# A state-space scan with attention and experts on one core: the chunk's head reordered, row scales stored once and loaded, the weights loaded in three groups

## What is computed

```python
xn = layernorm(x)                                   # mean and variance of each row
out = x + ssm(xn) + ffn(xn)                         # ffn: latent attention, then 7 experts, top 2

def ssm(x):                                         # D_MODEL 256, D_INNER 512, D_STATE 16
    x_in, z = split(x @ W_in)
    x_in = silu(causal_conv4(x_in, W_conv) + b_conv)
    dbc = x_in @ W_xproj                            # 64 columns for dt, 16 for B, 16 for C
    dt = softplus(dbc[:64] @ W_dt + b_dt)
    A = -exp(A_log)
    for t in range(512):
        state = clip(state * exp(clip(dt_t * A)) + x_t * dt_t * B_t, -10, 10)
        y_t = sum_n(state * C_t) + D * x_t
    return (y * silu(z)) @ W_out
```

## Time and profile before

| | us |
|---|---|
| median of three runs (4593.74 to 4607.09) | 4605.54 |
| profiled execution | 4602.04 |
| its span, first to last instruction | 4600.0 |
| span before the state-space part (first row load of it at 2195.09) | 2195 |
| first scan step | 2262.1 |
| end of the scan of chunk 30, start of that of chunk 31 | 4513.7 |

### The profile page before, as it was taken

The page is one execution under the profiler, slowest core; times in us unless marked ns, Lnnn a source line. Parts: engine busy times, 40 slices in busy tenths (PEclk is TensorE's granted clock), DMA queues, the critical chain, the costliest instruction groups (busy, mean ns, idle before and its releaser), DMA issues.

```text
span 4600.0 us, 72135 instructions
## 1 busy us (share of the span) xinstructions
PE 3800.7 (83%) x22840; PEld 2863.4 (62%) x22840; DVE 3006.1 (65%) x5613; ACT 2500.9 (54%) x6473; POOL 2243.8 (49%) x1251
## 2 busy tenths in 40 slices
PE   5888888888888857999588888888888888888886
PEld 2444444444444436777477777777777777777776
DVE  4445554454545322222399998888998989888887
ACT  1434444443434422333477776767767677776774
POOL 2233233333323220000376776777777777776774
PEclk8889999999989878999799999999999999999998
DMA  3222223322322216666222221222222222221221
GB/s 94 88 75 86 91 76 95 95 85 76 100 76 76 74 44 204 209 204 210 80 72 84 75 81 71 81 75 84 72 75 86 75 76 80 75 85 68 81 80 36
DMA packets 268587, 419.76 MB, mean 91 GB/s; under 512 B 60245, under 2 KB 232662, under 8 KB 245656
## 3 DMA queue, kind: packets, MB, share of 16 engines
q1 hardware_dynamic: 255896, 380.98, 25.7%
q0 software_dynamic: 12288, 33.57, 2.1%
HBM read 330.56 MB, written 83.10 MB: 90 GB/s over the span
## 4 chain that ended last, share of the span: by engine, by line
PE 16%; POOL 13%; ACT 9%; DVE 7%; issue 6%; DMA 1%; DVEq 0%; SPq 0%; POOLq 0%; ACTq 0%
POOL m_ub L1534 10%; PE m_Y L1902 7%; ACT m_dA L1652 6%; PE m_Y L1912 2%; PE m_F L1867 2%; PE m_F L1856 2%; DVE m_PR L1756 2%; POOL m_yg L1544 1%; DVE m_PR L1764 1%; DVE m_S L1756 1%; DVE m_S L1764 1%; PE m_Y L1915 1%; POOL m_dtx L1513 1%; PE m_F L1875 1%; DVE m_ub L1741 1%
## 5 line engine op out<-in xcount | busy, mean ns | idle before, releaser
L1534 POOL TENSOR_TENSOR m_ub<-m_Bb,m_dtx 128x2048 f32<-128x2048 f32 x256 | 1156.7, 4542 | 482.8 <-PE m_Y L1902 476.2
L1652 ACT ACTIVATE m_dA<-m_dt,m_a_neg 128x128 f32<-128x128 f32 x4096 | 1210.0, 389 | 27.3 <-DVE m_S L1764 23.4
L1902 PE MATMUL m_Y<-m_ub,m_ident 128*128 128x128 f32 x8192 | 1026.8, 290 | 222.1 <-DVE m_ub L1741 205.3
L1902 PEld LDWEIGHTS m_Y<-m_ub,m_ident 128*128 128x128 f32 x8192 | 1007.2, 206 | 232.0 <-DVE m_ub L1741 213.6
L531 ACT ACTIVATE f_pt<-f_X 128x512 f32<-128x512 f32 (+1 forms) x704 | 371.5, 554 | 723.4 <-PE f_X L822 692.0
L607 DVE TENSOR_REDUCE f_nm<-f_Y 128x1 f32<-128x512 f32 (+3 forms) x896 | 433.5, 530 | 364.5 <-PE f_Y L816 361.3
L1756 DVE SCALAR_TENSOR_TENSOR m_PR<-m_dA,m_S 128x512 f32<-128x512 f32 x512 | 355.8, 695 | 207.6 <-ACT m_dA L1652 84.0
L815 PE MATMUL f_Y<-f_kst,f_qst 96*128 96x512 bf16 (+3 forms) x1024 | 286.4, 335 | 104.9 <-DVE f_nm L607 87.8
L1756 DVE SCALAR_TENSOR_TENSOR m_S<-m_dA,m_PR 128x512 f32<-128x512 f32 x512 | 354.8, 693 | 12.0
L1764 DVE CUSTOM_DVE_ANT_1 m_S<-m_S,m_ub 128x512 f32<-128x512 f32 x512 | 353.3, 690 | 0.0
L1764 DVE CUSTOM_DVE_ANT_1 m_PR<-m_PR,m_ub 128x512 f32<-128x512 f32 x512 | 353.1, 690 | 0.2 <-DVE m_PR L1756 0.2
(11 more groups left out here) (238 smaller groups left out, 6622.9 us busy)
## 6 DMA issues: line engine op xcount, KB each, us to landing
m_Bb<-m_bc_dram SPq DMA_DIRECT2D x64, 1024.0 KB, 4.7
m_Cb<-m_bc_dram SPq DMA_DIRECT2D x64, 1024.0 KB, 4.7
f_parts_dram<-f_parts SPq DMA_DIRECT2D x32, 768.0 KB, 4.1
f_kst<-f_parts_dram SPq DMA_DIRECT2D x192, 128.0 KB, 2.6
f_qst<-f_parts_dram SPq DMA_DIRECT2D x192, 128.0 KB, 2.6
e_rows<-sorted_rows SPq DMA_DIRECT2D x70, 256.0 KB, 2.8
e_wg<-Wg SPq DMA_DIRECT2D x70, 256.0 KB, 2.9
e_wu<-Wu SPq DMA_DIRECT2D x70, 256.0 KB, 4.0
```

What stands on the lines that cost most here:

```text
L1534: pool.tensor_tensor(ub[:, h, i, :, :], Bb[:, s, :, :], dtx[:, par, m, None, s * SN:(s + 1) * SN].to_broadcast([P, NST, SN]), ALU.mult).th ...
L1652: last = act.activation(dA[:, h, i, n, :], dtt[:, par, m, s * SN:(s + 1) * SN], ACT.Exp, scale=a_neg[:, m, n:n + 1])
L1902: last = pe.matmul(Y[:, i * SN:(i + 1) * SN], ident[:, :], ub[:, h, i, n, :], start=False, stop=(n == NST - 1), skip_group_check=True)
```

## The change

The row scales (1 over the deviation, and minus the mean times that) are no longer worked out in the state-space part. `build_attn` has them already in `mvx`; SP stores them for every sequence (item `mvs`), and `load_x` loads them with the rows, two numbers a row. `stats` and `rstd_of` go. `load_x` is moved from the head of SP's chunk into `spread_bc`, three chunks ahead.

`project` is cut in two, `project_a` (the second half of x and the first of z, into F[2] and F[3]) and `project_b` (into F[1] and F[0]); `conv` is done in halves, the second half first. TensorE's list is now: sum of the last unit, `dbc`, `transposes`, output product, `dt_proj`, sum of unit 0, `project_a`, sum of unit 1, `project_b`, first half of `conv`, sum of unit 2, second half of `conv`. `transposes` write to F[0], and the output product goes to F[2] in place of Y. On ScalarE `normalise` stands first, and `evac_T` and the decays of unit 2 stand ahead of softplus. On VectorE silu comes at steps 3 and 4, the residual add at step 1 of unit 1, and `log_rest` at step 0 of unit 2. A new semaphore `d_done` tells `silu_x` that the skip term has read x2.

In the setup the loads have three semaphores: w_in, the columns for conv and skip, and the six others.

```diff
+            if kind == "mvs":
+                dst = at(rows_stat, b)
+                held(xn_done, 2 * b + 1)
+                with nc.allow_non_contiguous_dma(reason="two numbers of a row"):
+                    sp.dma_start(dst, mvx[:, :, :]).then_inc(mv_stored, 16)
...
-                dve.tensor_copy(mvx[:, 0, :], sc1[:, 1, :])
-                dve.tensor_copy(mvx[:, 1, :], sc1[:, 9, :]).then_inc(xn_done, 1)
+                dve.wait_ge(mv_stored, 16 * b)
+                dve.tensor_copy(mvx[:, :, 0], sc1[:, 1, :])
+                dve.tensor_copy(mvx[:, :, 1], sc1[:, 9, :]).then_inc(xn_done, 1)
...
+            with nc.allow_non_contiguous_dma(reason="two numbers of a row"):
+                sp.dma_start(rowsc[:, :, :], stat_tm[bass.ds(rows, CN), :].rearrange("(j p) d -> p j d", p=P)).then_inc(x_loaded, 16)
+
+        def spread_bc(c, ahead):
             for s in range(NSUB):
...
             for s in range(NSUB):
+                if s == NSUB - 1 and ahead is not None:
+                    load_x(ahead)
                 held(u_ready[2 * s + 1], 2 * c)
                 sp.dma_start(Bb[:, s, :, :], bc_dram[s:s + 1, 0, :, :].to_broadcast([P, NST, SN])).then_inc(b_loaded[s], 16)
...
         def chunk(c, par, rows_ahead=True):
-            if rows_ahead:
-                load_x(c + 2)
             store(c - 1)
             load_res(c)
             load_info(c + 1, 1 - par)
-            spread_bc(c + 1)
+            spread_bc(c + 1, c + 3 if rows_ahead else None)
 
         load_x(0)
-        load_info(0, 0)
+        sp.dma_start(w_in[:, :, :], W_in.rearrange("(k p) n -> p k n", p=P)).then_inc(w_in_loaded, 16)
+        with nc.allow_non_contiguous_dma(reason="per-channel columns, once"):
+            for k in range(TAPS):
+                sp.dma_start(w_cv[:, k, :], W_conv[k, :].rearrange("(m p) -> p m", p=P)).then_inc(cols_loaded, 16)
+            sp.dma_start(d_col[:, :], D.rearrange("(m p) -> p m", p=P)).then_inc(cols_loaded, 16)
         for dst, src in loads:
             sp.dma_start(dst, src).then_inc(w_loaded, 16)
-        with nc.allow_non_contiguous_dma(reason="per-channel columns, once"):
-            for k in range(TAPS):
-                sp.dma_start(w_cv[:, k, :], W_conv[k, :].rearrange("(m p) -> p m", p=P)).then_inc(w_loaded, 16)
-            sp.dma_start(d_col[:, :], D.rearrange("(m p) -> p m", p=P)).then_inc(w_loaded, 16)
+        load_info(0, 0)
         load_x(1)
-        spread_bc(0)
-        load_x(2)
+        spread_bc(0, 2)
...
-        def rstd_of(c):
-            pool.wait_ge(stats_done, TT * (c + 1))
-            pool.tensor_tensor(veps[:, :], mv[:, :, 1], eps[:, :], ALU.add).then_inc(veps_done, 1)
-            pool.wait_ge(veps_done, c + 1)
...
         def normalise(c):
-            act.wait_ge(shift_done, c + 1)
             act.wait_ge(xT_done, c)
-            act.wait_ge(x_loaded, 16 * (c + 1))
+            act.wait_ge(x_loaded, 32 * (c + 1))
             for j in range(TT):
-                act.activation(xn[:, j, :], xm[:, j, :], ACT.Identity, scale=rstd[:, j:j + 1],
-                               bias=shift[:, j:j + 1]).then_inc(xn_done, 1)
+                act.activation(xn[:, j, :], xm[:, j, :], ACT.Identity, scale=rowsc[:, j, 0:1],
+                               bias=rowsc[:, j, 1:2]).then_inc(xn_done, 1)
 
         def evac_T(c):
             act.wait_ge(xT_done, c + 1)
             act.wait_ge(xz_done, 4 * c)
-            act.activation(xnT[:, :, :], F[2][:, :, :], ACT.Copy).then_inc(xnT_ready, 1)
-
-        def evac_x(c):
+            act.activation(xnT[:, :, :], F[0][:, :, :], ACT.Copy).then_inc(xnT_ready, 1)
+
+        def evac_xz(c):
             act.wait_ge(conv_done, 2 * c)
             act.wait_ge(xpad_ready, 2 * c)
-            act.wait_ge(ident_ready, 5)
+            act.wait_ge(ident_ready, 4)
             if not isinstance(c, int) or c > 0:
 
                 act.activation(xpad[:, :, 0:HALO], xpad[:, :, CN:CN + HALO], ACT.Copy).then_inc(halo_done, 1)
                 act.wait_ge(halo_done, c)
             for i in range(2):
-                act.wait_ge(xz_done, 4 * c + i + 1)
-                act.activation(xpad[:, 2 * i:2 * i + 2, HALO:HALO + CN], F[1 + i][:, :, :], ACT.Copy).then_inc(xpad_ready, 1)
-
-        def tanh_z(c):
-            for i in range(2):
-                act.wait_ge(xz_done, 4 * c + 3 + i)
+                hx = 1 - i
+                act.wait_ge(xz_done, 4 * c + 2 * i + 1)
+                act.activation(xpad[:, 2 * hx:2 * hx + 2, HALO:HALO + CN], F[1 + hx][:, :, :], ACT.Copy).then_inc(xpad_ready, 1)
+                act.wait_ge(xz_done, 4 * c + 2 * i + 2)
...
-        act.wait_ge(setup_neg, 2)
         normalise(0)
         evac_T(0)
-        evac_x(0)
-        tanh_z(0)
+        act.wait_ge(w_loaded, 16 * 6)
+        act.activation(a_neg[:, :, :], a_neg[:, :, :], ACT.Exp).then_inc(setup_neg, 1)
+        evac_xz(0)
         tanh_x(0)
+        normalise(1)
         evac_dbc(0)
+        evac_T(1)
         softplus(0)
         ln(0)
+        act.wait_ge(setup_neg, 2)
         decays(0, 0, 0)
-        normalise(1)
-        evac_T(1)
-        evac_x(1)
-        tanh_z(1)
+        decays(0, 0, 1)
+        evac_xz(1)
         tanh_x(1)
-        decays(0, 0, 1)
 
         def body(c, par, first, last):
+            if has(c + 2):
+                normalise(c + 2)
+            if first:
+                decays(c, par, 2)
             if not last:
                 evac_dbc(c + 1)
+            if has(c + 2):
+                evac_T(c + 2)
+            if not first:
+                decays(c, par, 2)
+            if not last:
                 softplus(c + 1)
-            if has(c + 2):
-                normalise(c + 2)
-            decays(c, par, 2)
-            if not last:
                 ln(c + 1)
-                if has(c + 2):
-                    evac_T(c + 2)
             weigh(c, par)
             decays(c, par, 3)
+            if has(c + 2):
+                evac_xz(c + 2)
             if not last:
-                if has(c + 2):
-                    evac_x(c + 2)
-                    tanh_z(c + 2)
                 decays(c + 1, 1 - par, 0)
                 if has(c + 2):
                     tanh_x(c + 2)
...
-        def stats(c):
-            dve.wait_ge(x_loaded, 16 * (c + 1))
-            for j in range(TT):
...
-        def silu_x(c, par, halves=(0, 1)):
+        def silu_x(c, par, halves=(1, 0)):
             if not isinstance(c, int) or c >= 2:
-                dve.wait_ge(nsum_done[NU - 1], 2 * (c - 1))
+                dve.wait_ge(d_done, c - 1)
             for i in halves:
-                dve.wait_ge(thx_ready, 2 * c + i + 1)
+                dve.wait_ge(thx_ready, 2 * c + (1 - i) + 1)
...
-            dve.tensor_tensor(ot[:, :, :], Y[:, :].rearrange("p (j d) -> p j d", j=TT), res[:, :, :], ALU.add).then_inc(ot_done, 1)
...
+            dve.tensor_tensor(ot[:, :, :], F[2][:, :, :], res[:, :, :], ALU.add).then_inc(ot_done, 1)
...
             slots = [dict() for _ in range(NU)]
             if not first:
                 slots[0][5] = lambda: gate_y(c - 1, 1 - par, NU - 1)
-                slots[1][0] = lambda: add_res(c - 1)
+                slots[1][1] = lambda: add_res(c - 1)
             for u in range(1, NU):
                 slots[u][6] = lambda u=u: gate_y(c, par, u - 1)
             if not last:
-                slots[0][6] = lambda: silu_x(c + 1, 1 - par, [0])
-                slots[0][7] = lambda: silu_x(c + 1, 1 - par, [1])
-                slots[1][7] = lambda: log_rest(c + 1)
-            if has(c + 2):
-                slots[0][3] = lambda: stats(c + 2)
+                slots[1 if first else 0][3] = lambda: silu_x(c + 1, 1 - par, [1])
+                slots[1 if first else 0][4] = lambda: silu_x(c + 1, 1 - par, [0])
+                slots[2][0] = lambda: log_rest(c + 1)
...
         def transposes(c):
             pe.wait_ge(xn_done, TT * (c + 1))
-            pe.wait_ge(x2_ready, 2 * c)
+            if not isinstance(c, int) or c > 0:
+                pe.wait_ge(z_copied, 2 * c)
             for k in range(KM):
                 for j in range(TT):
-                    last = pe.transpose(F[2][:, k, j * P:(j + 1) * P], xn[:, j, k * P:(k + 1) * P], ident[:, :])
+                    last = pe.transpose(F[0][:, k, j * P:(j + 1) * P], xn[:, j, k * P:(k + 1) * P], ident[:, :])
             last.then_inc(xT_done, 1)
 
-        def project(c):
+        def project(c, i):
+            for m in range(2):
+                blk = 2 * i + m
+                for k in range(KM):
+                    last = pe.matmul(F[(1 + i) % 4][:, m, :], w_in[:, k, blk * P:(blk + 1) * P], xnT[:, k, :],
+                                     start=(k == 0), stop=(k == KM - 1))
+            last.then_inc(xz_done, 1)
+
+        def project_a(c):
             pe.wait_ge(xnT_ready, c + 1)
-            for i in range(4):
-                if i == 0:
-                    pe.wait_ge(sp_low, c)
-                if i == 1:
```

(84 more changed lines are left out.)

122 lines of the change are left out of this document (47 added, 75 removed).

## The result

The changed kernel took **4430.4 us** (median of 4 runs, 4412.2 to 4434.9) against 4601.9 us (median of 4 runs of the kernel before beside it): the ratio is 0.9606, with a 95% interval from 0.9574 to 0.9637. The forecast was 4441 us. The profiled execution of after took 4428.2 us, with a span of 4426.1.

A forecast was written before the change was run, and what follows sets the result against it. VectorE's scan, its own instructions plus its waits, was taken to bound the loop. Loop −134, start −12, first chunk −11 and last chunks and end −8 made −165 from 4602, plus 3.5: 4441 us, range 4398 to 4530.

The forecast's parts named there:

- The loop, −134 forecast: 28 looped chunks: 65.3 work, 1.35 wait ahead of unit 2, 1.2 edge; 67.8 us each against 72.6.
- with nothing to spare: Chunk's end: GpSimd's inputs of the next unit 0 end at +65.9, VectorE wants them at +66.1; the 1.10 us wait goes.
- it takes 7.3 like the sum at 3019.29: Chunk head, TensorE: sum of unit 3 starts at +1.4, takes 7.3 us and ends at +8.8.
- 1.2 edge: Chunk boundary: the loop's jump back, about 2.4 us at every second boundary, stays; 1.2 us per chunk on average.
- Rival B: TensorE at half clock ahead of the output product, or edge delays: 1.5 to 1.6 us more per chunk, 4486 us; chance 0.2.
- The start, −12 forecast: Setup: with three load groups x rows come first and conv starts 13.4 us earlier, less 1.3; 12 us taken.
- They now run ahead while VectorE waits: First chunk: projection and conv of chunk 1 no longer stand between its units; 70 us instead of 81.4, −11.
- Chunk 29 on, −8 forecast: Last three chunks and the end: no projection there; the head of each saves 2 to 3 us, −8.
- Ahead of the state-space part, 0 forecast: Attention part: 16 stores of small row-scale rows cost 0, bounds 0 to +10 us; no gain possible.
- D: Slower: late transposes (+18, not +12) hold the output product and unit 2; 73.7 us a chunk, 4662 us at 8 us; chance 0.04.
- E: The wait ahead of unit 2 vanishes too, or the edge is partly hidden: 38 us less, 4403 us; chance 0.06.
- C: GpSimd becomes the bound, late at unit 2 and the next unit 0: 70.4 us a chunk, 4512 us; chance 0.1.

The follow-up runs named there:

- e3: Changed kernel with TensorE running the output product ahead of dbc and the transposes again, as before: 4552.8 us, ratio 0.991.
- e5: Changed kernel with ScalarE's softplus of the next chunk ahead of the decays of unit 2 again: 4468.9 us, ratio 0.9728.
- e8: Changed kernel with skip-term matmuls repeated (six more times in unit 1, four in unit 3) to keep TensorE busy: 4416.9 us, ratio 0.9597.
- e4: Changed kernel with the old setup: all engines wait for every load, TensorE for all diagonals: 4466.0 us, ratio 0.9706.
- e10: Changed kernel with ScalarE's projection copies for chunk 1 ahead of the first decays, tanh_x between them: 4432.8 us, ratio 0.9644.
- e2: Changed kernel without the stored row scales: statistics worked out in the state-space part again, attention part as before: 4458.7 us, ratio 0.9702.
- e12: e11 with log_rest moved back to step 7 of unit 1: 4361.5 us, ratio 0.9515.
- e7: Changed kernel with four chunks per hardware loop pass instead of two, 7 jumps back instead of 14: 4426.5 us, ratio 0.9636.
- e11: Changed kernel with the edits of e7, e8 and e10 together: 4385.2 us, ratio 0.9547.

## Why the prediction was right

**The loop, −134 forecast, −137.1 measured.** (Unrounded, 28 times 72.57 less 67.85 is 132.) By its terms, from the step times of chunks 2 to 27: the work of 65.3 came to 65.0. Unit 2 waits 0.76 us and not 1.35: the 0.7 us that I added in every second chunk for a late ScalarE and TensorE behind the jump didn't come. The decays end 7.5 us early in every chunk, and GpSimd's inputs at +33.3 in either kind. The end of a chunk costs 1.46 and not 1.2: 28 × 0.26 = 7 us for GpSimd, which I had at +65.9 against VectorE's +66.1 "with nothing to spare", and which is at +66.1 in fact. Two waits of 0.2, at the end of units 0 and 2, were not in the sum. The errors, −0.3 and −0.6 against +0.26 and +0.4, nearly cancel: 67.8 forecast, 67.67 measured.

**The chain.** dbc's end was forecast at +11.7 and is +12.1 in the median; the decays of unit 2 at +16.6 to +26 ran from +16.55 to +26.0; the inputs of unit 2 at +24.6 to +33.6 ran from +24.3 to +33.3; the sum of unit 2 starts at +52.7 for +53.0, and the inputs of the next unit 0 run from +57.1 to +66.1 for +56.9 to +65.9. The residual add waits no more. e3 shows that this chain is the cause. e5 shows that the new place of the decays adds 19.3 us; without it 117.8 of the 137.1 us are still there.

**A step that failed at a small price:** "it takes 7.3 like the sum at 3019.29", of the sum of unit 3. It takes 8.7 us on average (9.04 in chunk 10), because the clock is often low behind its gap at the boundary, which I hadn't priced. Behind a jump back the gap is 3.4 to 4.8 us, and all 13 of these sums are slow (8.8 to 10.3 us). Elsewhere it is 2.0 to 2.4 us, and 5 sums of 15 are slow; in chunk 2 the same gap as in chunk 10 was followed by a sum at full speed.

```profile
2378.83 7.41 PE L1870 MATMUL m_Y<-m_ub,m_ident 128*128 128x128 f32 x64 [2.10 <-DVE m_ub L1705]
```

The windows view of after, at the sum in chunk 10 and behind the jump that ends this chunk:

```profile
2918.60:2922.60 4.00, 3.97 (x24) 3.97 (x25) 3.93 (x7) 4.00 (x15) 0.00 (x0) 0.69 0.74 229
2985.30:2992.00 6.70, 5.32 (x26) 5.33 (x27) 6.57 (x11) 6.70 (x24) 0.00 (x0) 0.52 0.39 159
```

0.69 and 0.52 of full clock, where 0.5 is the lower of its two levels, 1.2 GHz. It did no harm at unit 2, because dbc and the transposes still end at 2929.83, 0.5 us ahead of the output product. Its price, with that of the slow sum of unit 1, is read from e8: the waits of 0.2 us at the end of units 0 and 2 shrink to under 0.05 above a plain step, and the end of a chunk costs 0.3 less. So the term "1.2 edge" was short by what the low clock does to GpSimd's inputs. Rival B put this place at the output product; the low clock that is left stands where it costs less, 190.2 us of the loop for 279.9 before. The rule of the Trainium skill that B drew on (TensorE: Matmul & The Clock Gate, HAM oscillation) agrees with the gaps behind the jumps (13 sums of 13 slow) and in the main with those of 3.2 us ahead of the sums of unit 1 (23 of 28 slow, 9.02 us on average), but at 2.0 to 2.4 us 5 sums of 15 are slow, and the 0.48 us ahead of the output product stays at full clock, as I had assumed.

**The start, −12 forecast, −12.0 measured;** e4 gives 12.4 for the loads and the diagonals alone, and leaves open whether 5 us of chunk 0 belong to them too.

**Chunk 0, −11 forecast, −6.2 measured.** The step that failed is "They now run ahead while VectorE waits". Projection did, conv didn't. TensorE and ScalarE of after there:

```profile
2218.23 3.69 PE L1806 MATMUL m_F<-m_xnT,m_w_in 128*128 128x256 f32 x16 [0.97 <-DVE m_sp_v L1697]
2245.53 1.22 PE L1830 MATMUL m_F<-m_dt_in,m_b_cv 1*128 1x256 f32 x2 [23.61 <-ACT m_xpad L1577]
...
2258.71 7.31 PE L1870 MATMUL m_Y<-m_ub,m_ident 128*128 128x128 f32 x64
```

```profile
2225.80 18.80 ACT L1626 ACTIVATE m_dA<-m_dt,m_a_neg 128x128 f32<-128x128 f32 x64
```

conv of chunk 1 stands still for 23.61 us, until ScalarE has done 64 decays and gets to its copies; its first group then runs slow (3.78 us for 1.99), and the sum of unit 0, behind it in TensorE's order, starts at 2258.7 though its operands were ready some 6 us sooner. I had followed TensorE's queue and not ScalarE's. e10 puts that right and gets 2.6 of the 5 us; the rest stays open.

**Chunk 29 on, −8 forecast, −4.5 measured:** chunk 29 gained 3.5 us, but chunk 30 only 0.1 (68.5 to 68.3) and what follows 0.8, where I had put 2 to 3 us on each. Why wasn't looked into.

**Ahead of the state-space part, 0 forecast, −14.1 measured,** and not explained by the change. Its first instruction on GpSimd, in after, e2 (which has the attention part of the kernel before) and e4 (which has that of after):

```profile
2180.87 0.20 POOL L1469 MEMSET m_ident<- 128x128 f32 x1 [467.59 <-POOLq L1998]
```

```profile
2180.95 0.20 POOL L1470 MEMSET m_ident<- 128x128 f32 x1 [470.28 <-POOLq L2036]
```

```profile
2205.69 0.20 POOL L1469 MEMSET m_ident<- 128x128 f32 x1 [472.22 <-POOLq L2002]
```

With the store or without it, it starts between 2168 and 2210 us in the 14 profiled executions; that is a spread between executions, and part of the spans' difference is luck: it more than covers the 8.3 us by which chunk 0 and the end fell short. With the −14.1 taken out, the profiled difference is −160 for the −165 forecast. What sets the spread was not looked into.

**The other rivals.** D needed the transposes at +18; they start at +11.9. E needed the wait ahead of unit 2 or the jump to go; neither went, though e12 shows what it's worth when the first does.

The range, 4398 to 4530, needn't have reached so far up: GpSimd as the bound (C) was 82 us above the result, and only 0.2 to 0.3 us a chunk of its mechanism came true, at the boundary.

## What to carry to other kernels

Where the engine that bounds a loop waits once per pass, follow the chain back through every queue and ask at each in-order engine which work that is ready stands behind work that isn't; three lines of order on TensorE were worth 118 us here. Then work out what is next, to the tenth: the decays needed their own move (0.7 us a chunk), and the same move of log_rest into a wait was worth 3 us at most while GpSimd bound the end of the chunk and 24 us once it didn't. A moved step must be followed on every engine that feeds it, not only on its own.

## What the hardware showed that I had not expected

Matmuls that compute nothing new made the loop shorter: with gaps of 3.2 us filled to 0.5, the sums of unit 1 behind them took 7.41 us for 9.02, the low clock fell from 190.2 to 38.5 us in the loop, and the loop by 16.8 us. For the whole kernel the gain is clear only with e7's and e10's edits beside it (e11, 0.9547). The jump back costs VectorE 2.2 to 2.6 us at every place in these traces where it is what VectorE waits for, and 7 jumps fewer gave 18.5 us in e7 and 16.3 between e8 and e11. The loops of two kernels that differ in nothing inside the loop (after and e4) differed by 12 us, and what lies ahead of it by up to 42 us between executions, so a stage's difference of some 10 us in single profiles proves nothing here.
